# One level of Strassen's algorithm in the FFN products of a one-core transformer layer

## The reference

```python
x = x + attn(layernorm(x))          # one head, d = 256, over 2048 tokens of each of 2 sequences
n = layernorm(x)
h  = relu(n @ up_w) ** 2            # 1024 -> 2048
shared = h @ down_w                 # 2048 -> 1024
lat = n @ fc1_w                     # 1024 -> 512
r = sum(top2(n @ gate_w))           # one number for each token
routed = ((lat @ expert_w) * r) @ fc2_w      # 512 -> 512 -> 1024
x = x + layernorm(shared + routed) * gamma + beta
```

## Time and profile before

| | |
|---|---|
| time, median of 3 runs | 2774.43 us (2770.37 to 2774.5) |
| span of the profiled execution | 2773.3 us |
| TensorE matmul busy | 2574.6 us, 93% of the span |
| DVE busy | 1499.6 us, 54% |
| ACT busy | 953.0 us, 34% |
| DMA traffic | 356.55 MB, mean 129 GB/s, 41.3% of 16 engines |
| granted TensorE clock, mean | 0.966 |

### The profile page before, as it was taken

The page is one execution under the profiler, slowest core; times in us unless marked ns, Lnnn a source line. Parts: engine busy times, 40 slices in busy tenths (PEclk is TensorE's granted clock), DMA queues, the critical chain, the costliest instruction groups (busy, mean ns, idle before and its releaser), DMA issues.

```text
span 2773.3 us, 29644 instructions
## 1 busy us (share of the span) xinstructions
PE 2574.6 (93%) x11656; PEld 2131.0 (77%) x11656; DVE 1499.6 (54%) x1910; ACT 953.0 (34%) x1307; POOL 243.4 (9%) x574
## 2 busy tenths in 40 slices
PE   7869799999999989999999999999999999999996
PEld 5758588888888767778777787877877787788884
DVE  4454527888886544664544455455445536644433
ACT  3111234666465322333233233323323323333320
POOL 1000000000110110110100101011010101100001
PEclk8979899999999999999999999999999999999998
DMA  5244531322242454444445445444544534453432
GB/s 182 86 138 144 153 98 54 112 72 80 81 134 95 140 154 140 145 144 140 133 150 150 128 153 151 130 137 142 157 135 138 158 127 145 142 139 120 132 98 84
DMA packets 213532, 356.55 MB, mean 129 GB/s; under 512 B 22032, under 2 KB 91792, under 8 KB 213008
## 3 DMA queue, kind: packets, MB, share of 16 engines
q1 hardware_dynamic: 213392, 354.66, 41.3%
HBM read 259.95 MB, written 65.27 MB: 117 GB/s over the span
## 4 chain that ended last, share of the span: by engine, by line
PE 42%; DMA 38%; DVE 11%; SPq 3%; POOL 2%; issue 2%; ACT 1%; DVEq 0%; ACTq 0%; POOLq 0%
PE psum L114 42%; DMA LA<-att_s 17%; DMA x1b_s<-LA 6%; DMA WRAW<-in_upfc_dram 6%; SPq L95 3%; DMA RES<-x1b_s 3%; DMA RAW<-in_x_dram 3%; DVE WL L102 3%; DMA v_s<-OUT 1%; DVE LX L102 1%; DVE st L192 1%; DVE RT L102 1%; DVE T L294 1%; DMA F2R<-in_fc_dram 1%; DMA STG<-v_s 1%
## 5 line engine op out<-in xcount | busy, mean ns | idle before, releaser
L99 ACT ACTIVATE WH<-WRAW 128x512 fp32r<-128x512 f32 x640 | 396.3, 628 | 1030.0 <-PE psum L114 497.0
L102 DVE TENSOR_TENSOR WL<-WRAW,WH 128x512 fp32r<-128x512 f32 x640 | 432.0, 686 | 487.3 <-ACT WH L99 487.1
L114 PE MATMUL psum<-XH,WH 128*128 128x512 f32 x1280 | 511.4, 400 | 49.9 <-DVE WL L102 49.6
L114 PE MATMUL psum<-WH,HH 128*128 128x512 f32 x1280 | 505.8, 395 | 35.5 <-DVE WL L102 35.4
L114 PE MATMUL psum<-XL,WH 128*128 128x512 f32 x1280 | 506.0, 395 | 0.0
L114 PE MATMUL psum<-XH,WL 128*128 128x512 f32 x1280 | 504.8, 394 | 0.0
L114 PE MATMUL psum<-WL,HH 128*128 128x512 f32 x1280 | 503.5, 393 | 0.0
L114 PE MATMUL psum<-WH,HL 128*128 128x512 f32 x1280 | 503.1, 393 | 0.0
L114 PEld LDWEIGHTS psum<-XH,WH 128*128 128x128 f32 x1280 | 244.2, 191 | 118.3 <-DVE WL L102 68.0
L114 PEld LDWEIGHTS psum<-WH,HH 128*128 128x128 f32 x1280 | 243.7, 190 | 92.8 <-DVE WL L102 42.4
L114 PEld LDWEIGHTS psum<-XH,WL 128*128 128x128 f32 x1280 | 244.7, 191 | 52.6
(11 more groups left out here) (189 smaller groups left out, 3555.0 us busy)
## 6 DMA issues: line engine op xcount, KB each, us to landing
WRAW<-in_upfc_dram SPq DMA_DIRECT2D x320, 256.0 KB, 6.8
WRAW<-in_dn_dram SPq DMA_DIRECT2D x256, 256.0 KB, 2.9
att_s<-ATT SPq DMA_DIRECT2D x32, 516.0 KB, 2.6
LA<-att_s SPq DMA_DIRECT2D x32, 516.0 KB
RAW<-in_x_dram SPq DMA_DIRECT2D x32, 512.0 KB
LX<-in_x_dram SPq DMA_DIRECT2D x32, 512.0 KB
x1b_s<-LA SPq DMA_DIRECT2D x32, 512.0 KB
XL<-T SPq DMA_DIRECT2D x128, 128.0 KB, 3.3
```

What stands on the lines that cost most here:

```text
L99: return act.put(lambda e: e.activation(o, i, f, **kw), *toks)
L102: return (q or dve).put(lambda e: e.tensor_tensor(o, a, b, op=op), *toks)
L114: return pe.put(lambda e: e.matmul(o, w, m, start=start, stop=stop, **kw), *toks, sig=sig)
```

## The change

Each of the two FFN products is done by Strassen's algorithm (the form with seven products) at one level, on 1024 tokens at a time. Operand matrices are cut in 2 x 2 quarters; seven products of sums of quarters take the place of eight products of quarters.

**Weights.** The sums of the weight quarters are the same for all tokens. They are formed once by `quad_tasks`, split once into high and low parts, and stored to scratch DRAM (`wu_s`, `wd_s`). A full job (width 512) loads four blocks of 128 x 512, forms four sums, and stores seven high and seven low blocks. 14 full jobs run in stage A from step g = 8 on, one every 4 steps, on two buffers; 12 half jobs (width 256) run in attention, one every 3 steps, on one buffer. The key and value loads that stood in stage A from step 53 on are moved to steps 61 and 76 on.

**Chunks.** 4 supergroups `s` of 1024 tokens, each 70 up chunks and 70 down chunks of 12 matmuls: 560 chunks. A chunk loads 512 KB, the high and the low part, straight into a ring of six `WR` buffers, five chunks ahead (`w_fill`); there is no split of weights in the FFN any more.

**Sums around the products.** `x_sum` forms the four sums of token quarters and `x_piece` splits the seven left operands. `u_evac` adds the up products out of PSUM into four quarter buffers `HB`, `finish` applies relu and square (both on ACT) or the routing factor (DVE). `h_sum12`, `h_sum4` and `h_op` form and split the left operands of the down products, seven chunks ahead. `z_evac` adds the down products into `ZR`.

**LN2** goes two groups at a time. Group 1's four tiles are planned in chunks 1, 4, 7 and 10, because supergroup 0 needs groups 0 and 1. The eight tiles of the next supergroup stand in the down half of the one before, 7 chunks apart, with single `LX` and `LA` buffers as before and the same `perm`. Transposed tiles go through DRAM (`xT_s`): 16 stores for each group in place of the 16 shuffles, and loads of 1 MB each.

**Output.** Residual loads (`RES`) and stores of `out` now take 128 contiguous rows each, not `perm`.

```diff
+    wu_s = nc.dram_tensor("wu_s", (7, 10, 128, 1024), F32).ap()
+    wd_s = nc.dram_tensor("wd_s", (7, 10, 128, 1024), F32).ap()
+    xT_s = nc.dram_tensor("xT_s", (8, 128, 4096), F32).ap()
...
+    def quad_tasks(kind, j, R, H, name, wd, hf, *free):
+        s = {}
+        cs = slice(wd * hf, wd * hf + wd)
+
+        def load():
+            if kind == "u":
+                for at_, r, c in ((0, 1, 0), (1, 0, 0), (2, 0, 1), (3, 1, 1)):
+                    for q in range(2):
+                        src = upfc[j, 2 * c + q].rearrange("p (k r n) -> r p k n", k=2, r=2)[r]
+                        to = R[:, at_, 256 * q:256 * q + 256].rearrange("p (k n) -> p k n", k=2)
+                        s["ld"] = dma(to, src, f"{name}l", *free)
+                return
+            for c, to in ((0, R[:, 1:3, :]), (1, R[:, 0:4:3, :])):
+                src = dn[c, 2 * j:2 * j + 2] if j < 8 else e2_s[c, 2 * j - 16:2 * j - 14]
+                s["ld"] = dma(to, src.rearrange("r p n -> p r n")[:, :, cs], f"{name}l", *free, *((t_e2st,) if j >= 8 else ()))
+
+        def sums():
+            a = lambda i: R[:, i, :]
+            if kind == "u":
+                k = TT(a(4), a(3), a(0), ALU.add, s["ld"])
+                k2 = TT(a(6), a(1), a(0), ALU.subtract)
+                k = TT(a(5), a(4), a(1), ALU.subtract, k)
+                s["s"] = TT(a(7), a(2), a(5), ALU.subtract, k)
+            else:
+                k = TT(a(4), a(0), a(1), ALU.subtract, s["ld"])
+                k2 = TT(a(6), a(3), a(0), ALU.subtract)
+                k = TT(a(5), a(3), a(4), ALU.subtract, k)
+                s["s"] = TT(a(7), a(2), a(5), ALU.subtract, k)
+
+        def high():
+            A(H[:, 0:4, :], R[:, 1:5, :], AF.Copy, s["s"], *free)
+            s["h"] = A(H[:, 4:7, :], R[:, 5:8, :], AF.Copy)
+
+        def low():
+            to = (wu_s if kind == "u" else wd_s)[:, j].rearrange("i p n -> p i n")
+            TT(R[:, 1:5, :].bitcast(F32R), R[:, 1:5, :], f(H[:, 0:4, :]), ALU.subtract, s["h"])
+            k = TT(R[:, 5:8, :].bitcast(F32R), R[:, 5:8, :], f(H[:, 4:7, :]), ALU.subtract)
+            a = dma(to[:, :, cs], f(H[:, :, :]), f"{name}h", s["h"])
+            b = dma(to[:, :, 512 + wd * hf:512 + wd * hf + wd], R[:, 1:8, :], f"{name}r", k)
+            quad_st[kind, j, hf] = quad_st[name] = (a, b)
+
...
     plan = Plan()
+    jobs = [("u", j) for j in range(10)] + [("d", j) for j in range(4)]
+    t_e2all = (t_e2[1, 3], t_e2st, f_sp[3, 1], e_sp[3])
+    quads = []
+    for m in range(8):
+        quads += [(b, 8 + 4 * b + 8 * m) for b in range(2) if m < 6 or b == 1]
+    for (kind, j), (b, g0) in zip(jobs, sorted(quads, key=lambda q: q[1])):
+        def run(kind=kind, j=j, b=b, g0=g0):
+            free = quad_st.get(f"q{b}", t_e2all)
+            for g, task in zip((0, 2, 3, 4), quad_tasks(kind, j, *QB[b], f"q{b}", 512, 0, *free)):
+                if g:
+                    plan.add(g0 + g, task)
+                else:
+                    task()
+        plan.add(g0, run)
...
+    for j, w in enumerate("kv"):
+        for k in range(8):
+            n = (61, 76)[j] + k
+            plan.add(n, kv_load, 0, w, k)
+            plan.add(n + 2, lambda w=w, k=k, j=j: kv_split(0, w, k, *quad_st[f"q{j}"]))
...
         def trans():
             ln2_tr[t, tt] = dve.put(lambda e: e.transpose(
-                T2[:, :, tt, :], LX[:, :].rearrange("p (j c) -> p j c", c=32)), s["n"], *t2_free)
+                T2[:, :, tt, :], LX[:, :].rearrange("p (j c) -> p j c", c=32)), s["n"], *t2_free,
+                *((xt_st[t - 1],) if t else ()))
+            if tt == 3:
+                for g in range(4):
+                    for m in range(4):
+                        src = T2[32 * g:32 * g + 32].rearrange("p (j m) t r -> p m j (t r)", m=4)[:, m]
+                        to = xT_s[t, 32 * m:32 * m + 32].rearrange("c (j g q) -> c g j q", g=4, q=128)[:, g]
+                        xt_st[t] = dma(to, src, "xt", ln2_tr[t, 3])
...
+        if n < 70:
+            p, j = SEQ_U[n]
+            src, kind = wu_s[U_AT[p], j], "u"
...
+            p, j = SEQ_D[n - 70]
+            src, kind = wd_s[D_AT[p], j], "d"
+        toks = [t for hf in range(2) for t in quad_st.get((kind, j, hf), ())] if s == 0 else []
+        k = w_slot(c)
+        if k in w_free:
+            toks += w_free[k]
...
+    filled = [0]
+
+    def w_fill(c):
+        while filled[0] <= min(c + (5 if c >= 10 else 4), 559):
+            w_load(filled[0])
+            filled[0] += 1
...
+        def run(m=m):
+            free = quad_st.get("qc", t2_first)
+            for g, task in zip((0, 1, 1, 2), quad_tasks("d", 4 + m // 2, *QC, "qc", 256, m % 2, *free)):
+                if g:
+                    plan.add(3 * m + g, task)
+                else:
+                    task()
+        plan.add(3 * m, run)
...
+    def u_evac(s, p, kp, b):
+        A_, B_, C_, D_ = (q[:, kp] for q in quarters(s))
+        k, src = up_pe[s, p, 2 * kp + 1], pair(b)
...
+            t = p1_t[s, kp] = A(B_, src, AF.Copy, k, *u_free(s, "B", kp))
+        elif p == 2:
+            t = TT(A_, B_, src, ALU.add, k, p1_t[s, kp], *u_free(s, "A", kp))
+            hA[s, kp] = finish(s, A_, 0, kp, t)
+        elif p == 6:
+            t = q_t[s, kp] = TT(B_, B_, src, ALU.add, k, p1_t[s, kp])
+        elif p == 7:
+            t = v_t[s, kp] = TT(C_, B_, src, ALU.add, k, q_t[s, kp], *u_free(s, "C", kp))
+        elif p == 4:
+            t = TT(D_, C_, src, ALU.add, k, v_t[s, kp], *u_free(s, "D", kp))
+            hD[s, kp] = finish(s, D_, 0, kp, t)
+        elif p == 5:
+            t = TT(C_, C_, src, ALU.add, k, v_t[s, kp])
+            hC[s, kp] = finish(s, C_, 1, kp, t)
+            t = u4_t[s, kp] = TT(B_, B_, src, ALU.add, k, q_t[s, kp])
...
+    def u_chunk(s, n):
+        c = 140 * s + n
+        p, j = SEQ_U[n]
+        b = u_bank(s, n)
+        w, x = WR[w_slot(c)], xs_slot(s, XNAME[p])
+        o = bank(b)
+        for kt in range(4):
+            toks = [w_ld[c], x_sp[s, XNAME[p], kt // 2], *bank_free[b]]
+            ws = slice(128 * kt, 128 * kt + 128)
+            mm(o, w[:, 0, ws], x[0][:, kt, :], kt == 0, False, *toks)
+            mm(o, w[:, 0, ws], x[1][:, kt, :], False, False)
+            k = mm(o, w[:, 1, ws], x[0][:, kt, :], False, kt == 3, sig=(kt == 3))
+        up_pe[s, p, j] = k
+        w_free[w_slot(c)] = (k,)
+        if j % 2:
+            u_evac(s, p, j // 2, b - 1)
+
+    def h_sum12(s, kp):
+        A_, B_, C_, D_ = quarters(s)
+        s1_t[s, kp] = TT(B_[:, kp], B_[:, kp], C_[:, kp], ALU.add, hB[s, kp], hC[s, kp])
+        s2_t[s, kp] = TT(A_[:, kp], B_[:, kp], A_[:, kp], ALU.subtract, s1_t[s, kp], op_t[s, 1, kp])
+
+    def h_sum4(s, kp):
+        A_, B_, C_, D_ = quarters(s)
+        s4d_t[s, kp] = TT(D_[:, kp], D_[:, kp], A_[:, kp], ALU.subtract, s2_t[s, kp], op_t[s, 2, kp])
+
+    def ring(s, m):
...
+    def h_op(s, m):
+        p, kp = PRODS[m // 5], m % 5
+        A_, B_, C_, D_ = quarters(s)
+        hi, lo, raw = ring(s, m)
+        if m >= 4:
+            free = dn_pe[s, PRODS[(m - 4) // 5], 2 * ((m - 4) % 5) + 1]
+        else:
+            free = up_pe[s, (7, 4)[m // 2], 9]
+        src, tok = {1: (A_, hA), 2: (D_, hD), 6: (A_, s2_t), 7: (C_, hC), 4: (C_, hC), 5: (B_, s1_t), 3: (D_, s4d_t)}[p]
+        src, k = src[:, kp], tok[s, kp]
+        if p == 7:
+            k = TT(raw[:, :, :], src, A_[:, kp], ALU.subtract, k, s2_t[s, kp], free)
+            src = raw[:, :, :]
+        a = A(hi[:, :, :], src, AF.Copy, k, free)
+        op_t[s, p, kp] = TT(lo[:, :, :], src, f(hi[:, :, :]), ALU.subtract, a)
+
+    z_t, z_free = {}, {}
...
+    def d_tile(s, n, tt, sig):
+        c = 140 * s + 70 + n
+        p, kt = SEQ_D[n]
+        b = d_bank(s, p) + tt
+        w = WR[w_slot(c)]
+        hi, lo, _ = ring(s, 5 * PRODS.index(p) + kt // 2)
+        toks = [w_ld[c], op_t[s, p, kt // 2]]
+        if kt == 0:
+            toks += bank_free[b]
+        ts_ = slice(128 * tt, 128 * tt + 128)
+        mm(bank(b), hi[:, kt % 2, ts_], w[:, 0, :], kt == 0, False, *toks)
+        mm(bank(b), hi[:, kt % 2, ts_], w[:, 1, :], False, False)
+        k = mm(bank(b), lo[:, kt % 2, ts_], w[:, 0, :], False, kt == 9, sig=sig)
+        if sig:
+            dn_pe[s, p, kt] = k
+            w_free[w_slot(c)] = (k,)
+        return k
...
+    def res_load(s, r, tt, *toks):
+        res_ld[s, r, tt] = dma(RES[tt % 2][:, :, :], x1b_s[rows(s, r, tt)].rearrange("p (a n) -> p a n", a=2), f"res{tt % 2}",
+                               *(x1b_st[2 * s + r, q] for q in range(4)), *res_free.get(tt % 2, ()), *toks)
...
+                ln2_at(1 + 3 * tt, 1, tt, (LX, LA, BO, T2, None), (0, 1, 1, 1, 1, 1, 1, 2, 2, 2, 2))
+            for r in range(2):
+                plan.add(15, x_load, 0, 1, r, lambda: (pv_t[7, 7],))
...
+        plan.add(u + 16, gate_bc, 2 * s, u_bank(s, 20))
+        plan.add(u + 28, gate_bc, 2 * s + 1, u_bank(s, 32))
+        for m in range(35):
+            plan.add(d + 2 * m - 7, h_op, s, m)
```

(98 more changed lines are left out.)

478 lines of the change are left out of this document (232 added, 246 removed).

## The result

| | before | after |
|---|---|---|
| time, median | 2774.47 us (2770.37 to 2781.84) | 3179.23 us (3176.31 to 3186.97) |
| ratio, 95% interval | | 1.1461 (1.1438 to 1.1484) |
| span of the profiled execution | 2773.3 us | 3179.6 us |

The change makes the kernel 14.6% slower. The forecast was 2905 us with a range to 3040: the direction was right, the size wrong, and the time lies outside the range. The page of the kernel after says where to look: TensorE has 115 us less to do than in the earlier trace rows, but it is busy for 77% of a longer span.

A forecast was written before the change was run, and what follows sets the result against it. It took TensorE, 93% busy, to be held back by `perm` transfers on 4 of 16 DMA engines. 2773.3 + 180 (stage A) + 12 (attention) + 60 (FFN start) - 120 (chunk 20 on) = 2905 us; range 2700 to 3040.

The forecast's parts named there:

- What bounds the kernel: Whole kernel before: TensorE busy 93%, FFN paced by LN2's loop, stage A likewise bound; `perm` transfers use 4 of 16 engines.
- Stage A, +180: Stage A: twelve weight jobs in four groups add 167 us, last two jobs and moved key and value loads 13.
- Down halves, 82 us of loss each: Down halves 0 to 2: LN2's eight tiles at a 30.5 us period hold PE, 246 us in all.
- PE has to stop at chunk 62: Down halves: operands last to chunk 61; chunk 62, due at 168.6 us, starts at 251 behind the eighth tile's addition.
- SP is held too: Down halves: weight loads for chunk 62 on stand behind the store of the eighth LN2 tile.
- Matmuls and the rest of the FFN: 640 chunks become 560, 217.6 us less; added DVE work and weight stream hidden in up halves; tail about 10 us.
- The 5 us for small gaps: FFN from chunk 20 on: 5 us added to matmuls, down-half losses and tail, giving 1730 us.
- Attention, +12: Attention: half jobs add 10.3 us of DVE work a block; +12 us, 0 if gaps fill, +46 if none do.
- Start of the FFN, +60: First 20 chunks: supergroup 0 waits for group 1's LN2, stores, loads and sums; +60 us (+15 to +80).
- Rival 1: LN2's loop doesn't hold PE in the down halves, so the 246 us vanish: 2659 us, chance 0.15.
- rival 2: Stage A takes the jobs into its idle DMA share, +57 in place of +180: 2782 us, chance 0.13.
- Rival 3: Jobs run one after another in stage A, +310 us: 3035 us, chance 0.21.

The follow-up runs named there:

- run 2: Kernel before, with every transfer through `perm` (`RAW`, `LX`, `LA`, `x1b_s`, `RES`, output) issued as four transfers of 32 rows: 2532.37 us.
- run 1: Kernel after, with `RAW`, `LX`, `LA` and `x1b_s` transfers each issued as four transfers of 32 rows: 2688.79 us.
- run 7: Kernel after, with those transfers cut in four and 12 of 14 full and all 12 half weight jobs left out: 2503.41 us.
- Run 3: Kernel after, transfers whole, with 12 of the 14 full weight jobs and all 12 half jobs left out: 2978.02 us.
- run 8: run 1 with the 12 later stage A jobs loading and storing the same bytes but without their VectorE and ScalarE work: 2682.67 us, single execution.
- Run 5: Kernel after, with only LN2's transfers (`LX`, `LA`, `x1b_s`) cut into four of 32 rows, `RAW` left whole: 2792.63 us.
- Run 4: Kernel after, with the low parts of the weights not loaded in the down halves, 256 KB a chunk instead of 512: 3101.17 us, single execution.
- run 6: Kernel after, with the whole `LX` and `LA` loads of the down halves issued by GpSimd on its own queue instead of SP: 3271.02 us.
- run 10: run 1 with the roundings of attention's half jobs (`QHc` on ScalarE) one step later than their sums: 2660.65 us, single execution.
- run 9: run 1 with LN2's four tiles in attention started four steps apart instead of five: 2674.07 us, single execution.

## Why the prediction was wrong, by its steps

| | A | attention | chunks 0 to 19 | from chunk 20 |
|---|---|---|---|---|
| before | 434.0 | 404.1 | 83.2 | 1852.0 |
| before, cut (run 2) | 340.9 | 403.1 | 83.2 | 1703.0 |
| after | 599.4 | 499.8 | 165.9 | 1914.5 |
| after, cut (run 1) | 494.8 | 478.9 | 123.3 | 1585.7 |
| after, cut, no jobs (run 7) | 358.3 | 433.6 | 122.7 | 1586.4 |

**What bounds the kernel: right, and used too little.** The four engines were found in the trace of before; cutting the transfers gains 8.6% there and 490 us in after. No view tells the 16 engines apart: that it is four is worked out from rate and share, and the gain of the cut agrees.

**Stage A, +180: right** (+165.4; a group takes 80.5 us where 82.4 was worked out, DMA share 0.75). Run 3 confirms that it is the jobs (149.0 us). Why they cost this in after is argued from the prices and the share; run 8 shows that it is their transfers only where all transfers are cut. There stage A pays 153.9 us for the change with all 16 engines full, so the price doesn't hang on the four.

**Down halves, 82 us of loss each: this step failed.** It measured 132 to 137, some 51 more in each. Two things were wrong in it. The smaller is the size of the period: 35.0 us in the mean (34 to 36 between tiles of the first group, 31 to 32 in the second, 46 to 49 across the 16 stores), where I took 30.5 from a range to 33, and 10 for the stores. So the eighth tile's addition of `BO` comes 263 to 265 us into the half and not 244, which makes some 20 of the 51 us.

The rest is the path. What failed is "PE has to stop at chunk 62": I let PE run ahead to the last operands made. In the trace PE stops at every tile, for weights. One turn of the loop carries 7 chunks of the plan, that is 19.04 us of matmuls, so eight turns of 35.0 lose 8 x 15.96 = 128 us. The `WR` loads are issued behind `LA` and land behind it, and the ring of six holds 16.3 us of work, less than the 26.6 us from the store's issue to the addition. So PE stands before chunk 57 when I had it before 62. It starts again there at 276 to 277 us and not at 251, has 13 chunks left in place of 8, and loses another 11 to 14 us in them. I had written that "SP is held too", but only for chunk 62 on.

Run 5 shows the cause as far as it goes: with the order in SP's list unchanged and the transfers cut, a half loses 26 to 27 us. Run 4 shows that of a turn 3 us are the weights' bytes beside `LA`. Whether the weights come late more by SP's order behind a long transfer or by sharing engines with it stays open, as run 6 changed neither alone.

**Matmuls and the rest of the FFN: right in kind.** Up halves take 191 to 196 us (190 to 195 said). The tail took 14 us, not 10. The 5 us for small gaps measured some 30: 7 in what is left of the first up half, 11 in the others, 13 in the fourth down half, which has no LN2 beside it. With the loop out of the way (run 1), from chunk 20 on 1585.7 us against the 1469 of pure matmuls; the three down halves still lose 26 us each.

**Attention, +12: failed.** I costed the jobs as DVE work in DVE's gaps (at most +46). DVE had the room, but ACT, in order, waited for DVE's sums in every job (run 10 gives back 30 us of attention), and LN2's last tile with its 16 `xT_s` stores, ahead of the `ATT` stores on SP, stopped the output products (run 9 gives back 20 us of the 27 lost there in run 1). A step that is placed in a plan has a second price on each in-order queue it touches, and I had priced only the first.

**Start of the FFN, +60: mechanism right, size past the upper bound** (+82.7). Chunk 20 starts with PE idle for 11 us behind the sums, as said. The term's own sum gives 64, and chunk 20 stood at 921.3 before, not at 924. Cut, the stage takes 123.3 us (121.5 with LN2's transfers alone cut, run 5): 43 us of it were LN2's whole transfers.

**Rivals.** Rival 1 (LN2's loop doesn't hold PE) and rival 2 (stage A absorbs the jobs) are false in after. Rival 1 nearly holds once the transfers are cut: the period is then 21.9 us in the mean, below the 24.2 named. Rival 2 stays false even then, +153.9 us. Rival 3 (+310) is false.

**What is left open.** Run 7 shows that of 217.6 us of saved matmuls 77 arrive behind chunk 0 (1709.1 against 1786.2). The rest goes to the start (some 40 us more than the first 20 chunks take before), the three down halves (3 x 26), the fourth (13) and small gaps in the up halves; the tail is the same 13 us in both. In the second down half of run 5 PE waits for `WR` in three places, and the two longest waits (12.0 and 7.2 us) stand right behind the two sets of 16 `xT_s` stores, each of which takes SP over 10 us to issue. The first:

```profile
1842.93 10.55 SPq L95 DMA_DIRECT2D xT_s<-XT  x16
1858.04 1.22 PE L122 MATMUL psum<-WR,RG01h 128*128 128x512 f32 x2 [11.97 <-DMA WR<-wd_s]
```

No run moved these stores.
